# Cross attention over the context: all four out tiles of the group in front first, all four queries of the next group last

## The reference, cut to what matters

```python
q = (x @ Wq.T)                    # 32 heads of 128
k = (ctx @ Wk.T); v = (ctx @ Wv.T)  # 8 key/value heads of 128
q = _rmsnorm(q, q_norm_w)
k = _rmsnorm(repeat(k, 4), k_norm_w); v = repeat(v, 4)
scores = einsum('bhqd,bhkd->bhqk', q, k) / sqrt(128) + mask
probs = softmax(scores)
out = einsum('bhqk,bhkd->bhqd', probs, v) -> (b, q, 4096) @ Wo.T
x = _layernorm(x + out)
```

## Time and profile before

| | |
|---|---|
| time, median of 3 runs | 1472.35 us (1470.19 to 1472.77) |
| the profiled execution | 1467.15 us |
| its span | 1465.0 us |
| mean granted clock of TensorE | 0.991 |
| PE, PEld, DVE, ACT, POOL busy | 96%, 80%, 74%, 58%, 41% |

### The profile page before, as it was taken

The page is one execution under the profiler, slowest core; times in us unless marked ns, Lnnn a source line. Parts: engine busy times, 40 slices in busy tenths (PEclk is TensorE's granted clock), DMA queues, the critical chain, the costliest instruction groups (busy, mean ns, idle before and its releaser), DMA issues.

```text
span 1465.0 us, 24269 instructions
## 1 busy us (share of the span) xinstructions
PE 1407.8 (96%) x7610; PEld 1167.8 (80%) x7610; DVE 1090.4 (74%) x2485; ACT 854.6 (58%) x2146; POOL 604.5 (41%) x633
## 2 busy tenths in 40 slices
PE   7999999999989989999999999879999999999997
PEld 6788888887778867787778778668888888888873
DVE  5697667697688877767776776767788788788884
ACT  4556555655223157656755755648677677677660
POOL 4555444444022137556655745435243243242110
PEclk9999999999999999999999999999999999999999
DMA  8011110102122341330321321310111022012000
GB/s 323 1 73 72 73 63 9 72 33 102 58 87 87 114 135 55 103 128 30 130 100 47 111 101 58 129 73 30 40 63 73 15 73 86 15 72 78 1 0 29
DMA packets 30133, 107.72 MB, mean 74 GB/s; under 512 B 3847, under 2 KB 13191, under 8 KB 22104
## 3 DMA queue, kind: packets, MB, share of 16 engines
q1 hardware_dynamic: 30040, 106.58, 20.1%
HBM read 97.07 MB, written 9.50 MB: 73 GB/s over the span
## 4 chain that ended last, share of the span: by engine, by line
PE 53%; DVE 17%; issue 16%; POOL 8%; ACT 4%; DMA 1%; POOLq 0%; DVEq 0%; SPq 0%; ACTq 0%
PE bank L186 11%; PE bank L187 10%; PE bank L188 10%; PE bank L1774 3%; POOL yss L1407 2%; PE bank L316 2%; PE bank L1789 2%; PE bank L339 2%; PE bank L1795 2%; PE bank L1791 2%; POOL tmp L159 1%; PE bank L1231 1%; PE bank L1732 1%; PE bank L327 1%; PE bank L285 1%
## 5 line engine op out<-in xcount | busy, mean ns | idle before, releaser
L159 POOL TENSOR_TENSOR tmp<-tmp,sin 128x512 f32<-128x512 f32 x80 | 111.5, 1394 | 211.2 <-ACT tmp L152 211.2
L188 PE MATMUL bank<-wo_low,att_high 128*128 128x512 f32 x384 | 150.7, 392 | 0.0
L2073 DVE SCALAR_TENSOR_TENSOR logit<-bank,qss,amask 128x512 f32<-128x512 f32 x128 | 90.9, 747 | 57.0 <-PE bank L188 55.9
L1986 POOL TENSOR_TENSOR qss<-qss,half 128x4 f32<-128x4 f32 x32 | 34.9, 1090 | 199.6 <-DVE qss L2059 199.6
L1607 PE MATMUL bank<-kT,wg 128*128 128x256 f32 x512 | 113.1, 383 | 4.0 <-ACT prob L1641 4.0
L1893 ACT ACTIVATE prob<-logit,rmax 128x512 f32<-128x512 f32 x128 | 91.6, 719 | 37.8 <-DVE rmax L2077 37.8
L1607 PEld LDWEIGHTS bank<-kT,wg 128*128 128x128 f32 x512 | 98.1, 192 | 17.9 <-ACT prob L1641 4.4
L186 PE MATMUL bank<-l_wo_high,att_high 128*128 128x512 f32 x256 | 104.7, 409 | 1.8 <-DVE att_low L1491 1.1
L187 PE MATMUL bank<-xT_high,wq_low 128*128 128x512 f32 x256 | 102.3, 400 | 0.0
L187 PE MATMUL bank<-l_wo_high,att_low 128*128 128x512 f32 x256 | 99.8, 390 | 0.0
L1907 ACT ACTIVATE p_high<-bank 128x512 fp32r<-128x512 f32 x128 | 70.1, 597 | 46.4 <-PE bank L1774 46.1
(11 more groups left out here) (270 smaller groups left out, 4414.1 us busy)
## 6 DMA issues: line engine op xcount, KB each, us to landing
wq<-in_l_wq SPq DMA_DIRECT2D x16, 1024.0 KB, 6.6
wo<-in_l_wo SPq DMA_DIRECT2D x16, 1024.0 KB, 5.0
wkv<-in_l_wkv SPq DMA_DIRECT2D x16, 512.0 KB, 5.7
wg<-in_l_wg SPq DMA_DIRECT2D x8, 1024.0 KB, 4.8
wq<-in_x_wq SPq DMA_DIRECT2D x8, 1024.0 KB, 7.2
wo<-in_x_wo SPq DMA_DIRECT2D x8, 1024.0 KB, 4.9
kT<-in_x_wkv SPq DMA_DIRECT2D x8, 512.0 KB, 4.2
kv_keys<-logit SPq DMA_DIRECT2D x8, 512.0 KB, 4.6
```

Source lines behind the costliest of these rows:

```text
L159: eng.tensor_tensor(halves(tmp[4 + j % 2]), halves(tmp[2 + j % 2]), per_batch(sin), ALU.mult).then_inc(sem(f"{l}_sinp"), 1)
L188: return eng.matmul(dst, a_high, b_low, start=False, stop=stop)
L2073: dve.scalar_tensor_tensor(logit[s % 2][:, c, :], bank[3 + c][:, :], qss[p][:, 1, h, 2 * b + c:2 * b + c + 1], amask[:, c, :], ALU.mult, A ...
```

## The change

- PE: in each group but the first, steps 0 to 3 carry the four out tiles of the group in front (`out_late` for all t). In each group but the last, steps 4 to 7 carry the four queries of the next group. Group 0 keeps its queries 2 and 3 in steps 0 and 1, the last group its tiles 0 and 1 in steps 6 and 7 (`out_early`).
- PE and DVE: column sums, q_low and query_mean of the next group's heads 0, 1, 2 in steps 5, 6, 7, and of head 3 in step 0; the residual adds in steps 1 to 4.
- ACT: two wq chunks of the next group in each of steps 0 and 1, in place of those in steps 6 and 7; wo chunks 0 | 1, 2 | 3 in steps 4 | 5 | 6, in the last group 0, 1 | 2 | 3; a query's copies in each of steps 4 to 7.
- POOL: its list in the order that follows.
- The waits for the banks of the fillers are adapted. The Sinkhorn's semaphores sink_in and sink_sum become one, sink_exp and sink_ln become one, dt_turn joins dt.

```diff
@@ -843,11 +843,11 @@
...
-                dve.tensor_tensor(t4, src, wide(mx), ALU.subtract).then_inc(sem("sink_in"), 1)
-                dve.wait_ge(sem("sink_exp"), side + 1)
+                dve.tensor_tensor(t4, src, wide(mx), ALU.subtract).then_inc(sem("sink_vector"), 1)
+                dve.wait_ge(sem("sink_scalar"), 2 * side + 1)
...
-                dve.tensor_reduce(vec4(zsm[:, 2, :]), t_lines, AX.X, ALU.add).then_inc(sem("sink_sum"), 1)
-                dve.wait_ge(sem("sink_ln"), side + 1)
+                dve.tensor_reduce(vec4(zsm[:, 2, :]), t_lines, AX.X, ALU.add).then_inc(sem("sink_vector"), 1)
+                dve.wait_ge(sem("sink_scalar"), 2 * side + 2)
...
@@ -973,10 +973,10 @@
...
-                act.wait_ge(sem("sink_in"), side + 1)
-                act.activation(z, z, ACT.Exp).then_inc(sem("sink_exp"), 1)
-                act.wait_ge(sem("sink_sum"), side + 1)
-                act.activation(zsm[:, 1, :], zsm[:, 2, :], ACT.Ln).then_inc(sem("sink_ln"), 1)
+                act.wait_ge(sem("sink_vector"), 2 * side + 1)
+                act.activation(z, z, ACT.Exp).then_inc(sem("sink_scalar"), 1)
+                act.wait_ge(sem("sink_vector"), 2 * side + 2)
+                act.activation(zsm[:, 1, :], zsm[:, 2, :], ACT.Ln).then_inc(sem("sink_scalar"), 1)
...
@@ -1081,7 +1081,7 @@
...
-            last.then_inc(sem("dt_turn"), 1)
+            last.then_inc(sem("dt"), 1)
...
@@ -1380,7 +1380,7 @@
...
-            act.wait_ge(sem("dt_turn"), 1)
+            act.wait_ge(sem("dt"), 2)
...
@@ -1797,38 +1797,46 @@
                     last.then_inc(sem("x_value"), 1)
 
                 def out_early(t):
-                    pe.wait_ge(sem("x_split"), x_wo_chunk(g, KC - 1, last_group))
+                    pe.wait_ge(sem("x_split"), x_wo_chunk(g, KC - 1, True))
                     pe.wait_ge(sem("att_low"), X_LOW + 8 * g + 4)
-                    if last_group:
-                        pe.wait_ge(sem("x_added"), 4 * g + t - 1)
+                    pe.wait_ge(sem("x_added"), 4 * g + t - 1)
+                    out_split(pe, "x", bank[t % 2], t, [0, 1, 2, 3], (wo_high, wo_low[p]))
+
+                def out_late(t):
+                    if t == 0:
+                        pe.wait_ge(sem("x_split"), x_wo_chunk(g - 1, KC - 1, False))
+                    pe.wait_ge(sem("att_low"), X_LOW + 8 * g - (4 if t < 2 else 0))
+                    if t < 2:
+                        pe.wait_ge(sem("x_qmean"), 4 * g + t + 3)
                     else:
-                        pe.wait_ge(sem("x_qmean"), 4 * n + t + 1)
-                    out_split(pe, "x", bank[t % 2], t, [0, 1, 2, 3], (wo_high, wo_low[p]))
-
-                def out_late(t):
-                    pe.wait_ge(sem("att_low"), X_LOW + 8 * g)
-                    pe.wait_ge(sem("x_qmean"), 4 * g + t + 1)
+                        pe.wait_ge(sem("x_added"), 4 * g - 5 + t)
                     out_split(pe, "x", bank[t % 2], t, [0, 1, 2, 3], (wo_high, wo_low[1 - p]))
+
+                def bank_free(h):
+                    if h >= 2:
+                        return "x_qmean", 4 * n + h - 1
+                    return ("x_qmean", h + 3) if first else ("x_added", 4 * g - 1 + h)
 
                 for s in range(STEPS):
                     scores(s)
                     if s or not first:
                         turn_probs(s - 1)
-                    if s < 2:
-                        query(g, p, s + 2, ("x_qmean", s + 1) if first else ("x_added", 4 * g - 3 + s))
-                    elif s < 4:
-                        if not first:
-                            out_late(s)
-                    elif s < 6:
-                        if not last_group:
-                            query(n, 1 - p, s - 4, ("x_qmean", s - 1) if first else ("x_added", 4 * g - 5 + s))
-                    else:
-                        out_early(s - 6)
-                        if not last_group:
+                    if first and s < 2:
+                        query(g, p, s + 2, ("x_qmean", s + 1))
+                    if not first and s < 4:
+                        out_late(s)
+                    if s >= 4 and not last_group:
+                        query(n, 1 - p, s - 4, bank_free(s - 4))
+                    if s >= 6:
+                        if last_group:
+                            out_early(s - 6)
+                        else:
                             turn_keys(n, 1 - p, s - 6, 16 * g + 2 * (s - 1) + s - 5)
-                    if s in (1, 2):
+                    if first and s in (1, 2):
                         query_sums(g, s + 1)
-                    if s in (5, 6) and not last_group:
+                    if s == 0 and not first:
+                        query_sums(g, 3)
+                    if s >= 5 and not last_group:
                         query_sums(n, s - 5)
                     if s or not first:
                         values(s - 1)
@@ -1930,25 +1938,20 @@
                     for c in chunks:
                         high_chunk(act, "x_high", wq_high[pm], wq[pm], c)
 
-                more = not isinstance(g, int) or g < NG - 2
                 for s in range(STEPS):
                     if s or not first:
                         turned(s - 1)
                     exps(s)
                     normalise(s)
-                    if first and s in (1, 2):
-                        if s == 1:
+                    if s < 2 and not last_group:
+                        if first and s == 0:
                             act.wait_ge(sem("l1_gate"), 4 * NG)
-                        query_weights(1, 1, (2 * s - 2, 2 * s - 1))
-                    if s == 4:
-                        out_weights((0, 1, 2))
-                    if s == 5:
-                        out_weights((3,))
-                    if s in (6, 7) and more:
-                        query_weights(g + 2, p, (2 * s - 12, 2 * s - 11))
-                    if s < 2:
+                        query_weights(n, 1 - p, (2 * s, 2 * s + 1))
+                    if s in (4, 5, 6):
+                        out_weights((((0, 1), (2,), (3,)) if last_group else ((0,), (1, 2), (3,)))[s - 4])
+                    if first and s < 2:
                         query(g, p, s + 2)
-                    if s in (4, 5) and not last_group:
+                    if s >= 4 and not last_group:
                         query(n, 1 - p, s - 4)
                     if s in (2, 3) and not last_group:
                         x_squares(act, n, 1 - p, s - 2)
@@ -2004,24 +2007,28 @@
                         pool.wait_ge(sem("x_high"), x_wq_chunk(m, c))
                         low_chunk(pool, "x_split", wq_high[pm], wq_low[pm], wq[pm], c)
 
+                n = g + 1
                 first = isinstance(g, int) and g == 0
-                query_pow(g, p, 2)
-                if first:
-                    query_weights(1, 1, (0, 1))
-                query_pow(g, p, 3)
-                if first:
-                    query_weights(1, 1, (2, 3))
                 if not last_group:
-                    low_values(g + 1, 1 - p)
-                    x_key_pow(pool, g + 1)
+                    if first:
+                        query_weights(1, 1, (0, 1))
+                        query_pow(0, 0, 2)
+                        query_pow(0, 0, 3)
+                        query_weights(1, 1, (2, 3))
+                    else:
+                        query_pow(g, p, 3)
+                        query_weights(n, 1 - p, (0, 1, 2, 3))
+                    low_values(n, 1 - p)
+                    x_key_pow(pool, n)
+                else:
+                    query_pow(g, p, 3)
                 out_weights((0, 1, 2))
                 if not last_group:
-                    query_pow(g + 1, 1 - p, 0)
+                    query_pow(n, 1 - p, 0)
                 out_weights((3,))
                 if not last_group:
-                    query_pow(g + 1, 1 - p, 1)
-                if not isinstance(g, int) or g < NG - 2:
-                    query_weights(g + 2, p, (0, 1, 2, 3))
+                    query_pow(n, 1 - p, 1)
+                    query_pow(n, 1 - p, 2)
 
             query_pow(0, 0, 0)
             query_pow(0, 0, 1)
@@ -2105,26 +2112,28 @@
 
                 for s in range(STEPS):
                     logits(s)
-                    if s in (1, 2):
+                    if first and s in (1, 2):
                         query_rest(g, p, s + 1)
-                    if s in (5, 6) and not last_group:
+                    if s == 0 and not first:
+                        query_rest(g, p, 3)
+                    if s >= 5 and not last_group:
                         query_rest(n, 1 - p, s - 5)
                     if s or not first:
                         probs_rest(s - 1)
                     if s >= 2 or not first:
                         low(s - 2)
-                    if s == 0 and not first:
-                        add(g - 1, 1)
-                    if s in (3, 4) and not first:
+                    if 1 <= s <= 4 and not first:
```

(30 more changed lines are left out.)

## The result

The changed kernel takes 1487.28 us (median of 4 runs, 1485.96 to 1488.03), the kernel before in the same comparison 1471.27 (4 runs, 1468.43 to 1472.77): ratio 1.011, 95% interval 1.0092 to 1.0129. It is slower, as forecast, but by 16.0 us and not 7.5, and above the range. The profiled execution took 1487.72 us (span 1485.6).

The account below looks back on a forecast made before the run. PE was taken as the bound, busy in 96% of the span. Terms -2.6 + 1.8 + 6.8 + 1.5 = +7.5 us took the profiled 1467.15 to 1474.65; with 5.2 for the median, 1479.9, range 1475.5 to 1484.0.

Parts of the forecast that it names:

- the late chunk: Last group: ACT rounds wo chunk 3 only in step 6, so PE's first out tile starts later: +6.8 us.
- rival 3: PE catches up after the last group's wait, or the chain had slack; 6.8 shrinks to about 2.5: about 1474, chance 0.10.
- The clock: PE's clock falls to half rate after the idle gap in the last group: +1.5 us.
- The k_low wait of step 0 goes: PE's six waits in step 0 for the second half of the next group's keys vanish: -2.6 us.
- The k_low wait in step 7 comes: ACT's copies delay the first keys half, so PE waits 0.26 us in step 7 of seven groups: +1.8 us.
- PE's fillers ... nothing: Out tiles, queries and column sums on PE only move, with number and size equal: no cost.
- they shift by the same 0.4 us ... but PE's need of them shifts by more: Step 7's logits and ACT's normalise come 0.4 us later, but PE needs them later still: no wait counted.
- The sign that I had named for being wrong: The time from one group to the next changes by more than 0.3 us.
- Rival 2: Step 7's k_low wait twice as long and a longer half-rate stretch: 1.8 + 1.4 us more, 1483.1, chance 0.14.

Follow-up runs that it names:

- experiment 4: The changed kernel with 28 idle matmuls on PE in the last group's gap, before the wait for the wo chunks: 1482.79 us, ratio 1.0082.
- Experiment 7: The kernel before, with ACT copying the transposed keys half before the two wq chunks in steps 6 and 7: 1469.89 us, ratio 0.9993.
- experiment 3: The kernel before, with only the last group's wo chunks rounded as in the changed kernel: 1480.78 us, ratio 1.0046.

## Why the prediction was wrong, point by point

- **Slower, and by the late chunk: right.** The tile came 6.88 us later against its step's scores, 6.8 forecast, and the kernel before with only this edit shows the same 7.49 us of idle. Nothing behind absorbed it, so rival 3 is out: from step 7 to the end both kernels take 46.8 us.
- **The clock: right.** 1.5 us forecast; the step lost 2.6, 1.8, 1.6 and 1.5 us by it in four profiles with the same wait (experiment 4). The changed kernel's profile, with 2.6, is the highest of them.
- **The k_low wait of step 0 goes: right**, 2.6 us. Experiment 7 removes the same six waits without any of the rest.
- **The k_low wait in step 7 comes: right, sized too low.** I put 0.26 us on it, by start times. The transposes started 0.32 to 0.40 us late, of which 0.16 to 0.24 shows as idle. In group 1, k_low started 0.91 us after the step's scores and not 0.86, and the transposes 0.89 us behind k_low's start and not 0.81. I had taken that distance from one row of group 2; in the six waits before it is 0.80 to 0.90. By the start of the second four transposes it is 2.6 us over the seven groups, against 1.8.
- **"PE's fillers ... nothing", and "they shift by the same 0.4 us ... but PE's need of them shifts by more": this is the step that failed.** I followed what waits for the logits and normalise of step 7, and left out p_low, which stands between them on DVE and for which PE's key transposes in step 7 wait, because both use bank 6. In the kernel before, p_low of step 6 started 3.66 us after step 7's first scores and was done 0.15 us before the key transposes began (1085.00 plus 1.28, and 1086.43):

```profile
1086.43 0.63 PE L1741 MATMUL bank<-ident,tmp 128*128 128x128 f32 x4
```

  That 0.15 us was no room to spare. In the changed kernel, where the key transposes do wait, they too start 0.15 us behind p_low's end (1093.16 plus 1.28, and 1094.59). So before, the signal came just when it was needed, and the list of waits does not show it. The change gave DVE a q_low in step 7 in place of the residual add, but the add came after p_low and q_low comes before it. Here are both DVE queues in step 7, before and after:

```profile
1083.87 1.22 DVE L2077 TENSOR_REDUCE rmax<-logit 128x2 f32<-128x1024 f32 x1
1085.00 1.28 DVE L2091 TENSOR_TENSOR p_low<-bank,p_high 128x512 fp32r<-128x512 f32 x2
1086.20 0.41 DVE L2100 TENSOR_TENSOR att_low<-bank,att_high 128x256 fp32r<-128x256 f32 x1
1086.53 0.68 DVE L222 TENSOR_TENSOR x<-x,bank 128x512 f32<-128x512 f32 x1
```

```profile
1091.43 1.22 DVE L2084 TENSOR_REDUCE rmax<-logit 128x2 f32<-128x1024 f32 x1
1092.57 0.68 DVE L2060 TENSOR_TENSOR q_low<-bank,q_high 128x512 fp32r<-128x512 f32 x1
1093.16 1.28 DVE L2098 TENSOR_TENSOR p_low<-bank,p_high 128x512 fp32r<-128x512 f32 x2
```

  p_low now starts 4.74 us after the scores, 1.08 later: 0.59 for q_low, and 0.49 for the late k_low. The key transposes start 6.17 us after them and not 5.09, later by the same 1.08. PE itself is 0.4 late by then, so 0.65 us of wait remain, seven times: 4.6 us that had no term in the sum. The sign that I had named for being wrong came with it: from group 1 to group 2 it takes 57.45 us and not 56.91, more than 0.3 longer.
- **The sum, mended by the profiles:** -2.6 + 2.6 + 4.6 + 6.9 + 2.6 = 14.1 us, or 13.0 with the shortest of the half-rate losses. The medians say 16.0, the interval 13.5 to 19.0. Four of the five terms were in the forecast, and without the 4.6 the measured time would have been some 1482.7 us (an estimate), inside the range. My sum looked at the fillers and column sums on PE and had no term for the swap on DVE of two instructions of equal length (0.59 us each) that stand on different sides of p_low.
- **The range** took the unforeseen between the groups as at most a doubled k_low wait. Rival 2 had the direction, and it named the wrong wait.

## What to carry to other kernels

When work changes its place in a step, compare each engine's queue position by position: two instructions of equal length are no even swap if one stood behind, and the other now stands ahead of, the instruction that another engine waits for next. Look first at signals that arrive just in time, because the profile of before does not list these as waits. The distance from the end of the one instruction to the start of the other finds them: where it is already as short as in a real wait (0.15 us here), there is no room. And the last iteration needs its own check whenever due times move: work that a steady group needs one group later may be needed by the last group at once.

## What the runs showed of the hardware

A gap on PE of 7.5 us cost more than its length: the work behind it ran at half rate (granted clock 0.53 from 1431 to 1438 us), 2.6 us more in one profile, 1.5 to 1.8 in three others with the very same wait, and nothing with PE kept at work in the gap (granted clock 1.00). The Trainium skill, TensorE: Matmul & The Clock Gate, Part 1, says that the default clock is the throttled one and that activity releases it; experiment 4 agrees.

What I had not expected is how much the half-rate stretches vary between executions of equal code. The kernel before and that of experiment 3 have the same instructions in these stretches (us, engines' busy time and count, granted clock, DMA share, GB/s); first before, then experiment 3:

```profile
960.00:975.00 15.00, 9.85 (x40) 7.58 (x39) 8.10 (x17) 4.52 (x14) 2.77 (x3) 0.77 0.36 141
975.00:990.00 15.00, 13.76 (x84) 11.73 (x83) 10.48 (x19) 10.13 (x21) 4.89 (x5) 1.00 0.14 40
```

```profile
960.00:975.00 15.00, 9.85 (x37) 7.57 (x36) 8.49 (x18) 3.43 (x12) 2.77 (x3) 0.67 0.37 141
975.00:990.00 15.00, 14.76 (x74) 12.34 (x73) 8.17 (x14) 8.60 (x17) 4.47 (x4) 0.87 0.10 36
```

Both came to the first projections of cross attention at half rate (0.43 us from matmul to matmul). In the kernel before they were soon at full rate and stayed there; in experiment 3 the half rate lasted until 975.3 and came back from 982.3 to 985.6, so that the query in step 0 of group 0 took 4.04 us instead of 2.78. The scatter of the runs goes with this. Of the 23 runs of the kernel before, the seven with a mean granted clock of 0.990 to 0.992 took 1467.23 to 1468.25 us, and the five with 0.982 or 0.983 took 1473.03 to 1474.19. For a comparison of a few microseconds it means that one profile against one profile misleads (20.6 us here against 16.0), and that steps have to be compared with steps, and runs with runs of equal granted clock where the change leaves the gaps on PE as they are.
